# Another order of the steps inside the four slots of the first attention block

## The reference

```python
# block 0: attention, 32 heads of 16, 8 key/value heads
q = x @ Wq + bq;  k = ctx @ Wk + bk;  v = ctx @ Wv + bv
attn = softmax(q k^T * 0.25 + mask);  out = (attn v) @ Wo + bo
x = layernorm(out + x) * gamma + beta
# block 1: a non-local block over the time axis of each batch element
g_x = Wg x + bg;  theta = Wtheta x + btheta;  phi = Wphi ctx + bphi
y = softmax(phi^T theta) g_x;  w_y = Wz y + bz
x = batchnorm(w_y) + x
```

## Time and profile before

| what | us |
|---|---|
| three runs, median | 4258.7 (4257.36 to 4264.97) |
| profiled execution, whole | 4252.37 |
| profiled execution, its span | 4250.3 |
| PE busy in the span | 3984.5 (94%) |
| DVE, ACT, POOL busy in the span | 2213.1, 1505.8, 1416.7 |
| granted clock of PE, mean | 0.976 |
| first block's turns in the loop and next to it | about 120 to 900 of the span |

### The profile page before, as it was taken

One profiled execution on the slowest core, in us unless ns is written; L12 is line 12 of the kernel. 1 busy time (PEld: TensorE's weight loads), 2 busy tenths in 40 slices (PEclk: granted clock), 3 DMA queues, 4 the chain that ended last, 5 costly groups with the idle time before them and its releaser, 6 DMA issues. The chain is left out here.

```text
span 4250.3 us, 78494 instructions
## 1 busy us (share of the span) xinstructions
PE 3984.5 (94%) x30176; PEld 2504.9 (59%) x30176; DVE 2213.1 (52%) x2705; ACT 1505.8 (35%) x2622; POOL 1416.7 (33%) x1178
## 2 busy tenths in 40 slices
PE   6999999996989999999999999986999999999998
PEld 5666666664666666666666666654545545545443
DVE  3666666663356666666666665325434434434420
ACT  2555555554233334443433443211322312222220
POOL 2333333342254555555555454102211211211210
PEclk8999999998999999999999999998999999999999
DMA  3221222212320001000001101133010110110100
GB/s 102 80 78 63 80 71 78 67 59 97 118 75 30 30 31 40 30 30 30 30 33 40 35 32 62 69 111 122 5 41 3 39 41 1 41 41 1 41 10 10
DMA packets 123612, 211.97 MB, mean 50 GB/s; under 512 B 19296, under 2 KB 39776, under 8 KB 121760
## 3 DMA queue, kind: packets, MB, share of 16 engines
q1 hardware_dynamic: 120736, 200.80, 13.7%
q10 hardware_dynamic: 2560, 6.29, 0.4%
HBM read 125.24 MB, written 67.11 MB: 45 GB/s over the span
## 5 line engine op out<-in xcount | busy, mean ns | idle before, releaser
L2116 PE MATMUL c_pR<-c_proj_w,c_fcT 128*128 128x512 f32 x1024 | 460.0, 597 | 7.2 <-PEq L1963 3.3
L2056 PE MATMUL c_pR<-s_Wfr,c_fc_w 128*128 128x512 f32 x1024 | 456.6, 596 | 6.5 <-issue 2.4
L718 POOL TENSOR_TENSOR a_S<-a_S,a_negmax 128x2048 f32<-128x2048 f32 x64 | 231.1, 3610 | 488.2 <-DVE a_negmax L652 488.2
L1642 DVE COPY_PREDICATED b_A<-b_mask,b_pS 128x2048 f32<-128x2048 uint32 x96 | 304.5, 3172 | 155.3 <-PE b_pS L1316 154.8
L1812 POOL TENSOR_TENSOR b_R<-b_R,b_Wh 128x512 f32<-128x512 f32 x192 | 221.8, 1155 | 446.3 <-PE b_pS L1316 446.3
L2056 PEld LDWEIGHTS c_pR<-s_Wfr,c_fc_w 128*128 128x128 f32 x1024 | 191.1, 190 | 245.6 <-issue 240.9
L2116 PEld LDWEIGHTS c_pR<-c_proj_w,c_fcT 128*128 128x128 f32 x1024 | 189.2, 190 | 235.3 <-issue 224.1
L2126 ACT ACTIVATE c_fcT<-c_pR,s_vec 128x512 f32<-128x512 f32 x128 | 88.0, 688 | 608.5 <-PE c_pR L2056 579.7
L2253 POOL TENSOR_TENSOR c_S<-c_S,c_negmax 128x1024 f32<-128x1024 f32 x64 | 121.4, 1897 | 523.4 <-DVE c_negmax L2199 523.4
L2227 DVE TENSOR_TENSOR c_res<-c_res,c_pR 128x512 f32<-128x512 f32 x128 | 88.0, 688 | 398.1 <-PE c_pR L2116 373.2
L1316 PEld LDWEIGHTS b_pS<-b_R,b_kT 32*128 32x128 f32 x6144 | 203.6, 196 | 128.8 <-issue 105.9
(11 more groups left out here) (262 smaller groups left out, 7808.6 us busy)
## 6 DMA issues: line engine op xcount, KB each, us to landing
a_c<-ctx SPq DMA_DIRECT2D x16, 512.0 KB, 3.8
a_x<-x SPq DMA_DIRECT2D x16, 512.0 KB, 4.8
a_kexp<-a_kT SPq DMA_DIRECT2D x512, 16.0 KB, 1.8
mid_cT<-a_cT SPq DMA_DIRECT2D x16, 512.0 KB, 2.7
a_xl<-x SPq DMA_DIRECT2D x32, 256.0 KB, 2.7
a_cl<-ctx SPq DMA_DIRECT2D x32, 256.0 KB, 3.1
mid_x<-a_xl SPq DMA_DIRECT2D x32, 256.0 KB, 3.1
mid_wy<-a_wy SPq DMA_DIRECT2D x32, 256.0 KB, 2.1
```

Of the source, the lines that this page charges most:

```text
L718: nc.gpsimd.tensor_tensor(S[n % 2][:, :, :], S[n % 2][:, :, :], negmax[n % 2][:, :].unsqueeze(2).to_broadcast([P, RH, T]), ALU.add)\
L1642: nc.vector.copy_predicated(A[:, :, :].rearrange("p q (n two h) -> p q n two h", two=2, h=h)[:, :, :, 1, :], masks[h][:, :].bitcast(U32).r ...
L2056: mm = nc.tensor.matmul(bank, w[:, c, at * P:at * P + P], src[:, c, :], start=(c == 0), stop=(c == KC - 1))
L2116: mm = nc.tensor.matmul(bank, fcT[part % 2][:, m, g * T:g * T + T], proj_w[:, KC * part + m, :], start=(m == 0), stop=(m == KC - 1))
```

## The change

The table `SLOTS` is written anew; nothing else changes. The set of steps and their pairs stay the same, and so does each instruction. In slot 0, xT moves from behind th0 to behind k, and xb1 (POOL only) ahead of fTb1. In slot 1, y1 moves ahead of ta0, v from ahead of n1 and pv0 to behind fr0, n1 behind pv0, and ta1 comes over from slot 2 to stand ahead of wy1. In slots 2 and 3, xb0 becomes the first step of slot 3 (for POOL it stays between sc2 and sc3), sc3 moves behind o0 and ta2, and n0 behind pv2.

```diff
-        [("sc0", 0), ("ta3", -1), ("cT", 1), ("tb3", -1), ("k", 1), ("fs1", -2), ("pv3", -1), ("th0", -1), ("xT", 1), ("fTa1", -2), ("fTb1", -2),
-         ("xb1", -1)],
-        [("sc1", 0), ("o1", -1), ("ta0", 0), ("y1", -2), ("tb0", 0), ("f0", -1), ("v", 1), ("n1", -1), ("pv0", 0), ("fr0", -1), ("wy1", -2)],
-        [("sc2", 0), ("ta1", 0), ("tb1", 0), ("q0", 1), ("fs0", -1), ("pv1", 0), ("th1", -1), ("fTa0", -1), ("fTb0", -1), ("xb0", 0)],
-        [("sc3", 0), ("o0", 0), ("ta2", 0), ("y0", -1), ("tb2", 0), ("f1", -1), ("q1", 1), ("n0", 0), ("pv2", 0), ("fr1", -1), ("wy0", -1)],
+        [("sc0", 0), ("ta3", -1), ("cT", 1), ("tb3", -1), ("k", 1), ("xT", 1), ("fs1", -2), ("pv3", -1), ("th0", -1), ("fTa1", -2), ("xb1", -1), ("fTb1", -2)],
+        [("sc1", 0), ("o1", -1), ("y1", -2), ("ta0", 0), ("tb0", 0), ("f0", -1), ("pv0", 0), ("n1", -1), ("fr0", -1), ("v", 1), ("ta1", 0), ("wy1", -2)],
+        [("sc2", 0), ("tb1", 0), ("q0", 1), ("fs0", -1), ("pv1", 0), ("th1", -1), ("fTa0", -1), ("fTb0", -1)],
+        [("xb0", 0), ("o0", 0), ("ta2", 0), ("sc3", 0), ("y0", -1), ("tb2", 0), ("f1", -1), ("q1", 1), ("pv2", 0), ("n0", 0), ("fr1", -1), ("wy0", -1)],
```

## The result

| | before | after |
|---|---|---|
| median of 8 runs each, one chip | 4259.12 us (4250.26 to 4264.97) | 4240.74 us (4236.88 to 4246.2) |
| profiled execution: time, span | 4252.37, 4250.3 us | 4240.03, 4238.0 us |
| mean granted clock | 0.976 | 0.975 |

The ratio is 0.9958, with a 95% interval of 0.9946 to 0.997: the change makes the kernel 0.4% faster. Medians differ by 18.4 us, the two profiled executions by 12.3. Forecast were 4255.0 us, a gain of 3.7, and a range that ended at 4249.

A forecast was written before the change was run, and what follows sets the result against it. PE's own instruction stream was taken as the bound, with only idle time to win: -5.3 + 1.3 + 0.7 + 0.6 - 1.0 = -3.7 us, from the median 4258.7 to 4255.0 us, range 4249 to 4266.

The forecast's parts named there:

- What bounds the stage: First block's repeating turns: PE's own instruction stream is the limit, its length unchanged by reordering; only idle time can be won.
- The wait for the exponentials: sc2 waits for f0's exponentials on ACT; ta1 put between removes 0.41 us in each of 13 turns, -5.3 us.
- The junctions: New neighbours of PE's steps, mainly transposes, cost 0.10 us a turn, bounds -0.3 and +0.3: +1.3 us.
- The rule on weight loads: By the skill's rule every load of these 128-row steps stands alone, so new order costs nothing there: sum -5.0.
- wy1's bank: Slot 1: wy1 waits until DVE has taken pv0 out, 0.05 us a turn, bounds 0 and 0.3: +0.7 us.
- sc3 behind o0 on DVE: Slot 3: masking sc3 before f1 fits by 0.06 us on DVE, 0.46 on PE: nothing, up to 0.5 us a turn.
- The slower rival: f1 waits for sc3's masking behind o0's late chain on DVE: 7 to 14 us more, 4262 to 4269; chance 0.1.
- n1, n0, y1, v at nothing: Moving v and n1 behind pv0, n0 behind pv2, y1 ahead of ta0 and tb0 was taken to cost nothing.
- The ramp: Start of the block: ta3 of turn 1 slips about 1.6 us behind POOL's shift, 0.9 comes back: +0.6 us.
- Turn 15: Last turn, without v: sc2 waits 2.27 us for the exponentials and ta1 fills 0.96 of it: -1.0 us.
- The clock: Five 2.5 us gaps ahead of sc0 stay; clock falls after them are redrawn, between -4.9 and +11 us.
- the cost side of ±0.3: Rival that the wait only moves, to wy1 or into 0.3 us of junctions: 3.3 us back, about 4258; chance 0.2.

The follow-up runs named there:

- ta1 alone: Kernel before with only ta1 moved from slot 2 to slot 1, ahead of wy1: 4245.75 us, ratio 0.9984.
- written-out pair: Kernel before and changed kernel, each with the first block's hardware loop written out, no jump: 4232.56 us (ratio 0.9943) and 4219.05 us (0.9912).
- sc3 alone: Kernel before with only sc3 moved from the front of slot 3 to behind o0 and ta2: 4254.53 us, ratio 1.0005.
- slot 1 alone: Kernel before with slot 1 in the changed kernel's order, but ta1 left in slot 2: 4257.23 us, ratio 1.0009.

## Why the prediction was wrong, step by step

- **What bounds the stage: half right.** PE's stream is the limit, and the other engines never took over. But "the change reorders and neither shortens nor lengthens" that stream is wrong: PE's busy time in 12 turns fell from 700.5 to 695.6 us. From that sentence came the whole ceiling of the forecast, namely that only idle time could be won.
- **The wait for the exponentials, -5.3 us: right.** ta1 alone takes 0.41 us off a turn and the wait from the view.
- **The junctions, +1.3 us: this is the step that failed.** I took +0.10 us a turn. In the written-out pair a turn gained 0.70 us, of which 0.41 are the wait, so the junctions gave -0.29: the sign was wrong and the value lay at the end of the bounds, which were ±0.3. 13 x 0.39 = 5.1 us lie in this term. I had read the 0.87 us of xT and the 0.96 us of ta2 as transposes beside transposes and transposes alone. But xT stood between th0 and fTa1, both on the whole array, and behind ta2 came y0, which is not the earlier trace rows. Read by that, the rows carry the other theory: xT in its new place, ahead of pv3, costs 0.97 (687.96 to 688.93), o0 costs 0.11 less and fTb0 0.09 less as neighbours than with sc3 between them, v 0.09 less ahead of ta1 than ahead of pv0. I had seen that single steps differ by up to 0.1 us and called it small; ten junctions were new.
- **The rule on weight loads.** The Trainium skill (TensorE: Matmul & The Clock Gate, Part 3, The mechanism) lets a weight load overlap running matmuls only where it goes to other rows of the array. From that I had worked out that order costs nothing at the junctions, and a sum of -5.0. The measured turns disagree with it as they do with my +1.3: the order at the junctions gave 0.29 us a turn, with as many weight loads.
- **wy1's bank, +0.7 us: nothing in the turns.** PE met no wait for it there. The tie that I feared is real in turn 15, where v isn't there to cover it, and in the run with wy0 ahead of pv2, where a like one cost 0.44 us a turn.
- **sc3 behind o0 on DVE: right, to a few hundredths.** f1 starts 0.46 us after the masking ends, the margin that was worked out. The slower rival never came.
- **n1, n0, y1, v at nothing: right in the sum, wrong in the reason for n0.** Ahead of pv2 it would cost 2.2 us in turn 1, as the run with sc3 alone shows.
- **The ramp, +0.6 us: wrong in sign.** ta3 of turn 1 does wait for POOL, by 0.91 us. (The terms of the prediction, 87.2 + 2.29 + 2.29 + 3.61, end at 95.4 us and give a slip of 1.4, not 1.6.)

```profile
87.61 1.15 PE L432 MATMUL a_pS<-a_kexp,a_qT 32*128 32x256 f32 x16 [0.39 <-issue]
89.67 1.09 PE L441 MATMUL a_pR<-a_ident,a_S 128*128 128x128 f32 x8 [0.91 <-POOL a_S L717]
```

  But by sc0 of turn 2 the changed kernel is 1.85 us ahead in the written-out pair, and 1.32 of it is there at sc0 of turn 0. The prediction said that none of the transfers which xT holds up was ending a wait of PE. That is wrong: sc0 of turn 0 waits for the spreads of k. PE before, then the written-out pair (before, after):

```profile
45.03 2.09 PE L433 MATMUL a_pS<-a_kexp,a_qT 32*128 32x256 f32 x16 [5.57 <-DMA a_kexp<-a_kT]
...
43.64 2.09 PE L422 MATMUL a_pS<-a_kexp,a_qT 32*128 32x256 f32 x16 [3.42 <-DMA a_kexp<-a_kT]
...
42.32 2.09 PE L422 MATMUL a_pS<-a_kexp,a_qT 32*128 32x256 f32 x16 [2.81 <-DMA a_kexp<-a_kT]
```

  SyncE issues the first spread at 22.02 us in the written-out kernel before and at 20.72 in the changed one, 23.42 and 21.53 with the loop, and in all 14 kernels this sc0 starts 21.6 us later. In the first turn xT no longer stands behind skipped fills of pv3 and th0. The issue also moves by itself from one execution to the next, so the gain is best taken from the means, 21.2 us in the seven kernels with xT behind k and 22.3 in the seven others: about 1.1 us of the 1.85. In the profiled loop kernels the ramp gives 5.5 us, 1.9 of it by sc0 of turn 0 and 3.4 in turn 0. The latter is most likely the clock of those executions, not the order. The windows view shows 0.80 over turn 0 before (47.9 us) and 0.88 after (44.4), and two kernels whose ramp was not touched (ta1 alone, slot 1 alone) took 43.6 and 44.1 us at 0.96. In the written-out pair (0.87 and 0.86) turn 0 gained 0.4 us.
- **Turn 15, -1.0 us: wrong.** sc2 has no wait there, but wy1 has one of 1.28 us, because its bank is emptied only after f0's maximum. PE, then DVE:

```profile
943.96 1.12 PE L546 MATMUL a_pR<-a_yT,a_wzT 128*128 128x512 f32 x2 [1.28 <-DVE a_attT L669]
...
945.02 1.15 PE L432 MATMUL a_pS<-a_kexp,a_qT 32*128 32x256 f32 x16
```

```profile
939.49 2.29 DVE L693 TENSOR_REDUCE a_nmax<-a_pS 128x4 f32<-128x2048 f32 x1 [2.77 <-PE a_pS L525]
941.70 1.75 DVE L667 RECIPROCAL a_rec<-a_pR 128x256 f32<-128x256 f32 x1
943.48 0.42 DVE L669 TENSOR_TENSOR a_attT<-a_pR,a_rec 128x256 f32<-128x256 f32 x1
```

  I had said that the bank is free at f0 + 6.6; here it is f0 + 6.4, but without v PE reaches wy1 nearly 2 us earlier. The tail as a whole is worth about nothing in the written-out pair.
- **The clock: the gaps as forecast, the draw against the change.** The five gaps stay, 12.4 us as in the earlier trace rows. In the profiled execution after, four of the five were followed by a granted clock of half, the lower of the two levels (1.2 GHz), against two before:

```profile
381.80 2.09 PE L432 MATMUL a_pS<-a_kexp,a_qT 32*128 32x256 f32 x16 [2.59 <-issue]
```

  The same 16 matmuls take 1.15 us at full clock. By the length of slot 0 (13.1 us undisturbed, 14.6 or 15.8 after a fall) the falls cost 7.2 us after and 4.2 before. They hid 3.0 us of the gain.

**The account.** From sc0 of turn 2 to sc0 of turn 15, 13 turns: 13 x 0.73 = 9.5 us gained, 3.0 lost to falls, which leaves 6.5, and 150.16 to 930.00 is 6.7 us longer than 144.68 to 917.85. The forecast's 3.7 and the 11.1 us of the written-out pair lie about 7.4 apart: 5.1 in the junctions, 2.4 in the ramp, 0.7 in wy1's bank, 0.1 in the tail, and -1.0 in turn 15. With the order's own effect of 11.1 us instead of 3.7, 4258.7 - 11.1 would have been 4247.6. The medians show more, 13.5 us in the written-out pair, 15.5 and 18.4 with the loop. What lies between 11.1 and these is not settled; the intervals of the ratios are about ±5 us wide, and the median of before moves by 6 us from chip to chip.

**The chances.** The result, 0.42% faster, fell where the prediction had put a chance of 0.1, but not in the way given there (all of PE's visible idle time and a kind clock together). The range left out everything below 4249 because no case had the stream itself become shorter. The lower bound of my own junction term would have opened it: -0.3 a turn instead of +0.1 is 5.2 us, 4249.8, and with fewer falls 4245. I had carried the cost side of ±0.3 into a rival and not the gain side.

## What to carry to other kernels

When PE's own stream is the limit and the work is only reordered, don't take that stream's length as fixed: sort its steps by what stands ahead of and behind them in the trace, compare starts of equal steps, and price the junctions both ways, as a rival of their own on each side. Put steps that use a part of the array side by side: here it gave some 0.1 us for each change saved, but only where no wait ate it. So cover the wait first (ta1), then gather the steps. A loop whose jump stops PE is worth writing out where the instructions allow it: here it gave more than the whole change of order.

## What the runs showed of the hardware that I had not expected

- The order of the same matmuls changes PE's time: 58.29 to 57.79 us in a turn, waits taken off, by 0.05 to 0.1 us for each change between steps on the whole array and steps on a part of it. The step on the whole array pays: o takes 3.43, 3.53 or 3.63 us with none, one or two such neighbours.
- The jump of a loop costs PE 2.2 to 2.9 us each pass, and in many passes (two to five of five) the granted clock falls to half right behind it, for another 1.4 to 2.8 us. Writing the loop out, with its five jumps, saved 4257.43 - 4232.56 = 24.9 us in the kernel before and 4241.93 - 4219.05 = 22.9 us in the changed one. Gaps (12.4) and falls (4 to 7) are 16 to 20 of that.
- Some 3 to 7 us more come from where no code was changed: from the first matmul of the second block to the end, eight kernels with the loop take 3201.1 to 3206.1 us, and the six written out 3198.3 to 3198.7. Part of the spread is the clock: over the first 200 us of this stretch it was 0.94 in the five kernels with the loop that took 3203.2 us or more, and 0.96 or 0.97 in the three that took 3201.1 to 3202.2 and in the six written-out ones. For the last 3 us the records show no cause, and it stays open.
